# The first layer of the edge network, moved from the edge loop into the stage of the six experts

## Chip, cores and metric

One core of one Trainium2 chip runs the whole program. The metric is the device time of one execution in microseconds (us), the median of three runs.

## What is computed

The reference is a graph network of two blocks on 3125 nodes with 256 features and 50,000 edges. Block one: linear attention, six steps of a gated graph network, and six dense experts. Block two: a Galerkin-type attention beside an edge convolution, then routed experts. The change concerns one line of the edge convolution, with `ele` (50,000 x 8), `fc_w0` (8 x 64) and `fc_w1` (64 x 256) all given as inputs:

```python
hid = jax.nn.silu(edge_length_embedded @ fc_w0 / np.sqrt(NB))   # first layer
w = hid @ fc_w1 / np.sqrt(RN)                                    # second layer
wA, wB, wC, wD = (w[:, :MUL], w[:, MUL:2 * MUL], w[:, 2 * MUL:3 * MUL], w[:, 3 * MUL:])
midA = wA * xs0 * sh0          # xs0, xs1: node rows gathered by edge_src
...
y0 = jax.ops.segment_sum(mid0, edge_dst, num_segments=Nn) * inv_nb
```

`hid` depends on inputs alone, so it can be made at any time ahead of the edge loop.

## The kernel before

The program is a chain of stages, each a function with one instruction stream per engine, set down in Python order; engines meet only through semaphores (`wait_ge`, `then_inc`), and a barrier of all engines ends each stage. An engine takes its instructions strictly in order, so a wait holds up all that is queued behind it. Products that must be close to fp32 are made from two parts (`PARTS`): a high part rounded to the fast type fp32r, and the rest as a low part.

**The expert stage** (`expert_mlp`, L1686) has 42 steps `i`: seven groups of 448 nodes (`GW`) times six experts. `layer1`, `layer2` and `layer3` (L1788 to L1818) are twelve products each of 448 columns, from L1784: three combinations of parts, two halves of 256 inputs, two halves of 256 outputs. TensorE's order in a step is `layer1(i+1)`, `layer2(i)`, `layer3(i-1)` (L1826 to L1835), so each layer's result has most of a step to become the next one's operand. ScalarE takes PSUM out through relu (L1853, L1864) and makes the high part of the first hidden layer (L1857); VectorE makes the low part (L1905), scales by the gate (L1910) and splits the second hidden layer (L1915, L1917). GpSimd makes the low parts of the 18 expert matrices at the start (L1772) and is then done. After each group ScalarE copies the sum out (L1871), and TensorE turns it node by node (L1823), up to one tile of 128 nodes per step, which VectorE adds to the rows (L1960). The sync queue SP loads expert matrices (L1735), each when the one four before it has been split, and for every step the gate row spread over 128 partitions (L1745), when the scaling three steps before is done.

**The stage before it** (`gnn_to_experts`, L1464) splits the 8 edge features into parts and stores them as 24 rows, high, low, high (L1514), to `ea8_dram`. **The stage behind it** (`norm_and_galerkin`, L1970) makes among other things the first layer's weights `fw0` (L2177 to L2188).

**The edge loop** (`edge_convolution`, L2217) goes over 98 units of 512 edges, each of four chunks of 128. For a unit: SP loads 24 x 512 edge features (L2276); TensorE makes the first layer in one product of 512 columns (`hidden`, L2305), whose 128 outputs are the 64 hidden values twice; ScalarE applies silu (L2413); VectorE rounds all 128 rows (L2457) and overwrites the lower 64 with the low part (L2459). For each chunk TensorE then makes the second layer with two products of 256 columns (`weights`, L2313). GpSimd gathers 128 node rows by an indirect DMA (L2288) into one of eight buffers. VectorE multiplies gathered rows and weights (L2482, L2483), ScalarE multiplies one-hot rows of the destinations by four edge attributes (L2421), and TensorE sums over edges by products with them (`sums`, L2325 and L2328; the fp32 type makes each of these two instructions). Once per unit ScalarE copies the sums (L2428), TensorE turns them (L2336), and VectorE adds them at their nodes (L2491). TensorE's order in unit `q` is `hidden(q+2)`, and for each chunk `sums(q, j)`, `weights(q+1, j)`, with the turn of the last unit behind the second chunk.

The next stage, `route_to_blocks`, begins with a square root on ScalarE (L2695).

## Time and profile before

| | us |
|---|---|
| timed runs, median of 3 (lowest, highest) | 3843.97 (3841.3, 3848.61) |
| the profiled execution, from its first to its last instruction | 3966.1 |
| the difference of the two | 122.1 |
| expert stage, start of the first and of the last layer product | 2167.9 to 2503.6 |
| edge loop, first load issued to start of the last turn | 2647.3 to 3354.7 |

The profile shows one execution, recorded by the hardware on the core. Its clock starts at its first instruction. PE is TensorE, PEld its weight loads, DVE VectorE, ACT ScalarE, POOL GpSimd, SP the sync engine's queue; L1784 is a line of the kernel. TensorE's products are pipelined: one starts before the one ahead of it has ended, so a price is read from the distance of starts or of ends, not from a duration. A bracket with "idle before" gives the time that the engine had stood still and what ended it.

### The profile page before, as it was taken

How to read it: one execution, taken by the hardware profiler on the slowest of the kernel's cores; microseconds unless marked ns; L12 is line 12 of the kernel's file. 1: busy time of each engine (PE TensorE's matmuls, PEld its weight loads, DVE VectorE, ACT ScalarE, POOL GpSimd, SP SyncE). 2: the span in 40 equal slices, each digit the busy share in tenths (PEclk: the TensorE clock that was granted, in tenths of full speed). 3: DMA queues.
4: the chain of work that ended last, by engine and by line, in shares of the span. 5: the costliest groups of instructions: out<-in, count | busy, mean ns of one | idle time of the engine just before them, and what ended most of it. 6: DMA issues, size and time to landing. Idle time of an engine off the chain costs nothing. (4 is left out here: it accounts for less than half of the span.)

```text
span 3966.1 us, 60201 instructions
## 1 busy us (share of the span) xinstructions
PE 3642.8 (92%) x18935; PEld 3087.8 (78%) x18935; DVE 2451.9 (62%) x4843; ACT 1491.9 (38%) x3475; POOL 665.9 (17%) x658
## 2 busy tenths in 40 slices
PE   5999899999999999999996999988888888869996
PEld 2555699999999998999994888657777777848885
DVE  7886655555555555556554666556666665677775
ACT  0363311211211111112114544457777775136663
POOL 0002000000000000000002200025555553012221
PEclk9999999999999999999997999989999999879998
DMA  1353022222222222222222210112222222431113
GB/s 53 65 105 65 26 87 89 65 89 84 70 84 74 80 88 71 83 83 71 83 69 98 72 31 30 42 47 83 81 84 79 84 80 59 150 71 38 38 38 119
DMA packets 265216, 288.48 MB, mean 73 GB/s; under 512 B 70331, under 2 KB 237327, under 8 KB 264283
## 3 DMA queue, kind: packets, MB, share of 16 engines
q1 hardware_dynamic: 233701, 208.44, 18.1%
q0 software_dynamic: 24192, 66.15, 5.8%
q10 hardware_dynamic: 7030, 10.16, 0.7%
q8 instruction: 162, 2.65, 0.3%
q14 instruction: 131, 1.07, 0.1%
HBM read 242.21 MB, written 42.48 MB: 72 GB/s over the span
## 5 line engine op out<-in xcount | busy, mean ns | idle before, releaser
L1043 PE MATMUL bank<-a_wide,parts 125*128 125x448 f32 x4200 | 872.9, 367 | 0.0
L1043 PEld LDWEIGHTS bank<-a_wide,parts 125*128 125x128 f32 x4200 | 785.6, 188 | 78.4 <-issue 9.9
L2288 POOL DMA_INDIRECT rows<-h_dram,src_t x392 | 375.4, 958 | 331.9 <-DVE prod L2483 218.7
L2421 ACT ACTIVATE hot<-eq,ea 128x80 f32<-128x80 f32 x1568 | 405.3, 352 | 1.0 <-DVE eq L2463 0.5
L1093 DVE CAST a_wide<-a_cols 125x2240 fp32r<-125x2240 bf16 x210 | 275.5, 1328 | 138.7 <-PE bank L1043 138.7
L1017 POOL TENSOR_TENSOR nf_g<-nf,nf_g 128x896 fp32r<-128x896 f32 x42 | 95.4, 2271 | 1575.0 <-ACT nf_g L1187 1575.0
L2328 PEld LDWEIGHTS bank<-prod,hot 128*80 128x80 f32 x2352 | 295.9, 153 | 70.9 <-issue 21.6
L2328 PE MATMUL bank<-prod,hot 128*80 128x128 f32 x2352 | 331.8, 277 | 10.6 <-issue 10.4
L1052 PE MATMUL bank<-nf_g,whh 128*128 128x448 f32 x1512 | 339.7, 369 | 0.0
L1052 PE MATMUL bank<-msg,wc 128*128 128x448 f32 x1512 | 339.1, 369 | 0.0
L1052 PEld LDWEIGHTS bank<-msg,wc 128*128 128x128 f32 x1512 | 284.2, 188 | 27.5
L1052 PEld LDWEIGHTS bank<-nf_g,whh 128*128 128x128 f32 x1512 | 284.3, 188 | 27.4
L1192 ACT ACTIVATE msg<-bank 128x448 fp32r<-128x448 f32 x84 | 41.1, 541 | 700.7 <-PE bank L1043 700.7
L2482 DVE TENSOR_TENSOR prod<-rows,bank 128x128 f32<-128x128 f32 x392 | 111.2, 284 | 231.0 <-PE bank L2313 198.4
L2325 PE MATMUL bank<-prod,hot 128*80 128x256 f32 x784 | 240.8, 389 | 11.3 <-ACT hot L2421 7.4
L3035 DVE TENSOR_TENSOR w_up<-w,w_up 128x912 fp32r<-128x912 f32 x168 | 184.8, 1101 | 106.8 <-ACT w_up L2977 106.8
L1147 DVE TENSOR_TENSOR msg<-bank,msg 128x448 fp32r<-128x448 f32 x84 | 48.6, 620 | 306.1 <-ACT msg L1192 306.1
L2924 PE MATMUL bank<-w_up,x_t 128*128 128x456 f32 (+1 forms) x1008 | 223.2, 375 | 3.2 <-DVE w_up L3035 2.7
L1784 PE MATMUL bank<-h,ew 128*128 128x448 f32 x1008 | 214.4, 367 | 1.3 <-DVE h L1917 1.3
L2483 DVE TENSOR_TENSOR prod<-rows,bank 128x384 f32<-128x384 f32 x392 | 214.4, 547 | 0.0
L2313 PE MATMUL bank<-fw,hid 128*128 128x256 f32 x784 | 193.8, 329 | 20.7 <-DVE hid L2459 15.3
L1784 PEld LDWEIGHTS bank<-h,ew 128*128 128x128 f32 x1008 | 188.7, 188 | 19.9 <-issue 3.9
(438 smaller groups left out, 5787.7 us busy)
## 6 DMA issues: line engine op xcount, KB each, us to landing
a_cols<-a_dram SPq DMA_DIRECT2D x210, 546.9 KB
a_dram<-a_cols SPq DMA_DIRECT2D x15, 1250.0 KB, 9.9
w<-in_w SPq DMA_DIRECT2D x4, 2728.0 KB
deg_bc<-deg_dram SPq DMA_DIRECT2D x42, 224.0 KB, 6.0
gate_bc<-gate_dram SPq DMA_DIRECT2D x42, 224.0 KB, 3.2
rows<-h_dram,src_t POOLq DMA_INDIRECT x392
w<-y_rows SPq DMA_DIRECT2D x12, 512.0 KB, 15.1
w<-in_w SPq DMA_DIRECT2D x6, 896.0 KB
```

The source lines that it names most:

```text
L1043: ins = nc.tensor.matmul(p_msg[f][:, 0:GW], parts[0:SPB, m, c * HB + k, f * 128:(f + 1) * 128], a_wide[u % 2][0:SPB, k, :], start=(c == 0 ...
L1052: ins = nc.tensor.matmul(out_p[:, 0:GW], w_m[:, k, part * D + f * 128:part * D + (f + 1) * 128], x_o[:, k, :], start=(start and c == 0), s ...
L1093: nc.vector.tensor_copy(a_wide[u % 2][0:SPB, :, :], a_cols[u % 3][0:SPB, :, :]).then_inc(a_done, 1)
L1784: ins = nc.tensor.matmul(to[f][:, 0:GW], w_p[:, m, k, f * 128:(f + 1) * 128], x_p[:, i % 2, k, :], start=start and c == 0, stop=stop and c ...
L2288: nc.gpsimd.indirect_dma_start(out=rows[n % ITC][:, :], out_offset=None, in_=h_dram, in_offset=bass.IndirectOffsetOnAxis(ap=src_t[:, n:n + ...
L2313: ins = nc.tensor.matmul(p_w[j][0:EC, 0:4 * MUL], hid[:, q % 2, j * EC:(j + 1) * EC], fw1[m][:, :], start=(m == 0), stop=(m == PARTS - 1))
L2325: nc.tensor.matmul(to[:, 0:4, :], hot[:, b, j, 0, :], p[:, 0:8:2, :], start=(j == 0), stop=False, skip_group_check=True)
L2328: ins = nc.tensor.matmul(to[:, 4 + c:8:3 - c, :], hot[:, b, j, 1 + c, :], p[:, 1:4 + 2 * c:2 + 2 * c, :], start=False, stop=(j == UC - 1 a ...
L2421: ins = nc.scalar.activation(hot[:, q % 2, j, m, :], eq[:, q % 2, j, :], ACT.Copy, scale=ea4[:, q * UC + j, m:m + 1])
L2483: nc.vector.tensor_tensor(slots[:, 2:8, :].rearrange("p (c a) u -> p c a u", a=2), xs1, w_cd, ALU.mult)\
L2924: ins = nc.tensor.matmul(p_h[i][:, 0:cut.stop - cut.start], x_t[x][:, n % 2, k, :], w_up[w][:, k, cut], start=(c == 0), stop=(c == len(ter ...
L3035: nc.vector.tensor_tensor(w_up[1][:, :, cuts[i]], w13[:, bass.ds(e, 1), :, cuts[i]].rearrange("p o k n -> p (o k) n"), w_up[0][:, :, cuts[ ...
```

## The change

The first layer of all 50,000 edges is made in the expert stage and stored; the edge loop loads it.

- 98 pieces, three in each step from step 5 to step 37 of the experts: one behind `layer1`, one behind `layer2`, one behind `layer3`, on TensorE and in matching places on ScalarE. A piece is 256 columns (`HE`) of a pair of units at once: 48 input rows (two units' 8 features in three part combinations) against a weight matrix with the units' blocks apart, 128 outputs (64 hidden values of each unit).
- Each piece: three loads (16 rows of 1 KB), a product in PSUM bank 7, two silus of it on ScalarE (one rounded, one not), a subtraction on GpSimd that leaves the low part, and a 256 KB store to `hid_dram`. There are two buffers `hid` and three of `ea`. TensorE waits for the silus of the piece before, ScalarE for the store of the piece before that one.
- Bank 7 is taken from the transposes, which use bank 6 alone until the last group.
- In the edge loop `hidden`, `silu` and `split` are gone. SP loads a unit in two DMAs of 128 KB into one of seven buffers, when the second layer of seven units before has been made.
- The weights `fw0` are split on GpSimd in the expert stage; their preparation on VectorE and three memsets on GpSimd leave the stage between. The edge features are stored as 16 rows, one store of 1.5 MB fewer.
- In the adjacency builder a count is held at zero or above by one more register instruction per tile.

```diff
+HIDS = 7
+HE = 256
+PIECES = 2 * NIT
+FIRST_STEP = 5
...
-        ea8_dram = nc.dram_tensor("ea8_dram", (3 * 8, NCH * EC), F32).ap()
+        ea8_dram = nc.dram_tensor("ea8_dram", (2 * 8, NCH * EC), F32).ap()
+        hid_dram = nc.dram_tensor("hid_dram", (NIT, PARTS, 128, UE), F32).ap()
...
-            ea8 = sb(ctx, "ea8", [128, 2, UE], F32R)
-            fw0 = sb(ctx, "fw0", [128, 128], F32R)
+            hid = sb(ctx, "hid", [128, HIDS, UE], F32R)
...
                         act.reg_alu(rounds, ranges_at[t // AHEAD % 2][t % AHEAD], PACK_BITS, ALU.arith_shift_right)
-                        act.reg_add(turns, turns, rounds)
+                        act.reg_alu(more, rounds, 0, ALU.max)
+                        act.reg_add(turns, turns, more)
...
-                for at_row, part, ready in ((0, 0, ea_high), (16, 0, ea_high), (8, 1, ea_low)):
+                for at_row, part, ready in ((0, 0, ea_high), (8, 1, ea_low)):
                     sp.wait_ge(ready, START + 1)
                     sp.dma_start(ea8_dram[at_row:at_row + 8, :].rearrange("a (p n) -> (a p) n", p=EP), ea_parts[part][:, :].bitcast(F32))\
                       .then_inc(ea_stored, 16)
-                sp.wait_ge(ea_stored, START + 48)
+                sp.wait_ge(ea_stored, START + 32)
...
+        ea = [sb(ctx, f"ea{b}", [48, HE], F32R) for b in range(3)]
+        fw_raw = sb(ctx, "fw_raw", [48, 128])
+        fw_high = sb(ctx, "fw_high", [48, 128], F32R)
+        fw = sb(ctx, "fw", [48, 128], F32R)
+        hid = sb(ctx, "hid", [128, 2, PARTS, HE], F32R)
+        gate_t = hid[0:NT, :, :, :].rearrange("p b m n -> p (b m n)").bitcast(F32)[:, 0:E0 * RT].rearrange("p (e n) -> p e n", n=RT)
...
+        def piece(i, spot):
+
+            n = 3 * (i - FIRST_STEP) + spot
+            return range(n, n + 1) if 0 <= n < PIECES else range(0)
+
+        def turned_in(t):
+            return p_x[0] if t < SOON else p_x[t % 2]
+
...
+                def edges(n):
+                    if n < PIECES:
+                        i, h = divmod(n, 2)
+                        units = ea8_dram.rearrange("(m a) (i u c) -> m i u a c", m=PARTS, i=NIT, u=2)[:, i, :, :, h * HE:(h + 1) * HE]
+                        sp.dma_start(ea[n % 3][0:16, :].bitcast(F32), units[0]).then_inc(ea_in[n % 3], 16)
+                        sp.dma_start(ea[n % 3][16:32, :].bitcast(F32), units[1]).then_inc(ea_in[n % 3], 16)
+                        sp.dma_start(ea[n % 3][32:48, :].bitcast(F32), units[0]).then_inc(ea_in[n % 3], 16)
+
+                def move(n):
+                    i, h = divmod(n, 2)
+                    sp.wait_ge(hid_mm, START + n + 1)
+                    edges(n + 3)
+                    sp.wait_ge(hid_low, START + n + 1)
+                    sp.dma_start(hid_dram[i, :, :, h * HE:(h + 1) * HE].rearrange("m p e -> p m e"), hid[:, n % 2, :, :].bitcast(F32))\
+                      .then_inc(hid_out[n % 2], 16)
...
+                sp.dma_start(fw_raw[:, :], A["fw0"]).then_inc(fw_in, 16)
+                for n in range(3):
+                    edges(n)
                 for m in range(8, NM):
                     weights(m)
-                for i in range(4, NI):
-                    gate_load(i)
+                for i in range(4, NI + 4):
+                    for n in piece(i - 4, 0):
+                        move(n)
+                    if i < NI:
+                        gate_load(i)
+                    for spot in (1, 2):
+                        for n in piece(i - 4, spot):
+                            move(n)
                     if i == WKV_AT:
                         sp.wait_ge(w_low, START + NM)
                         sp.dma_start(wkv[:, :, :], A["wkv1"].rearrange("(k p) n -> p k n", p=128)).then_inc(wkv_in, 16)
+                for b in range(2):
+                    sp.wait_ge(hid_out[b], START + PIECES // 2 * 16)
 
...
+                pool.wait_ge(fw_in, START + 16)
+                nc.gpsimd.tensor_copy(fw_high[:, :], fw_raw[:, :]).then_inc(fw_step, 1)
+                pool.wait_ge(fw_step, START + 1)
+                nc.gpsimd.tensor_tensor(fw[:, :], fw_raw[:, :], fw_high[:, :], ALU.subtract).then_inc(fw_step, 1)
+                pool.wait_ge(fw_step, START + 2)
+                nc.gpsimd.tensor_copy(fw[0:32, :], fw_raw[0:32, :]).then_inc(fw_step, 1)
+                for n in range(PIECES):
+                    pool.wait_ge(silu_done, START + n + 1)
+                    nc.gpsimd.tensor_tensor(hid[:, n % 2, 1, :], hid[:, n % 2, 1, :].bitcast(F32), hid[:, n % 2, 0, :], ALU.subtract)\
+                      .then_inc(hid_low, 1)
 
...
+                def edge_layer(n):
+                    pe.wait_ge(fw_step, START + 3)
+                    pe.wait_ge(gate_done, START + 1)
+                    pe.wait_ge(ea_in[n % 3], START + n // 3 * 48 + 48)
+                    pe.wait_ge(silu_done, START + n)
+                    nc.tensor.matmul(p_hid[:, 0:HE], fw[:, :], ea[n % 3][:, :], start=True, stop=True).then_inc(hid_mm, 1)
+
                 def turn(t):
-                    pe.wait_ge(added, START + t - 1)
+                    if t < SOON:
+                        pe.wait_ge(added, START + t)
+                    else:
+                        pe.wait_ge(added, START + t - 1)
+                        pe.wait_ge(silu_done, START + PIECES)
                     for k in range(KD):
-                        ins = nc.tensor.transpose(p_x[t % 2][0:RT, k * 128:(k + 1) * 128], xt[:, k, t * RT:(t + 1) * RT], ident[:, :])
+                        ins = nc.tensor.transpose(turned_in(t)[0:RT, k * 128:(k + 1) * 128], xt[:, k, t * RT:(t + 1) * RT], ident[:, :])
                     ins.then_inc(turned, 1)
...
+                    for n in piece(i, 0):
+                        edge_layer(n)
                     if i < NI:
                         layer2(i)
+                    for n in piece(i, 1):
+                        edge_layer(n)
                     if 0 < i <= NI:
                         layer3(i - 1)
+                    for n in piece(i, 2):
+                        edge_layer(n)
...
+                def edge_layer(n):
+                    act.wait_ge(gate_out, START + 64)
+                    act.wait_ge(hid_mm, START + n + 1)
+                    act.wait_ge(hid_out[n % 2], START + n // 2 * 16)
+                    for m in range(PARTS):
+                        to = hid[:, n % 2, m, :]
+                        ins = nc.scalar.activation(to if m == 0 else to.bitcast(F32), p_hid[:, 0:HE], ACT.Silu,
+                                                   scale=8.0 ** -0.5)
+                    ins.then_inc(silu_done, 1)
...
                     if i + 1 < NI:
                         hidden1(i + 1)
+                    for n in piece(i, 0):
+                        edge_layer(n)
                     if i < NI:
                         hidden2(i)
+                    for n in piece(i, 1):
+                        edge_layer(n)
...
+                    for n in piece(i, 2):
+                        edge_layer(n)
 
...
-                for t, name in ((fw0_raw, "fw0"), (fw1_raw, "fw1"), (ea4, "ea4")):
+                for t, name in ((fw1_raw, "fw1"), (ea4, "ea4")):
                     sp.dma_start(t[:], A[name]).then_inc(edge_in, 16)
...
-                nc.gpsimd.memset(fw0[:, :].bitcast(F32), 0.0).then_inc(rest_zero, 1)
-                for n in range(2):
-                    pool.wait_ge(d_mm, START + n + 1)
-                    nc.gpsimd.memset(ea8[:, n, :].bitcast(F32), 0.0)
...
                 rounds, regs = begin(sp, "sp", per_round)
                 with sp.Fori(0, rounds) as r:
-                    units, dmas = at_round(sp, regs, per_round)
+                    chunks, = at_round(sp, regs, per_round)
                     for q in range(NU):
-                        b = q % 2
-                        sp.wait_ge(hid_mm, units + q - 1)
-                        sp.dma_start(ea8[0:24, b, :].bitcast(F32), ea8_dram[:, q * UE:(q + 1) * UE]).then_inc(ea_in[b], 16)
+                        pair, u = divmod(q, 2)
+                        sp.wait_ge(w_mm, chunks + max(q - HIDS + 1, 0) * UC)
+                        for m in range(PARTS):
+                            sp.dma_start(hid[m * MUL:(m + 1) * MUL, q % HIDS, :].bitcast(F32),
+                                         hid_dram[pair, m, u * MUL:(u + 1) * MUL, :]).then_inc(hid_in[q % HIDS], 16)
...
-                    def hidden(q):
-                        b = q % 2
-                        pe.wait_ge(ea_in[b], dmas + (q // 2) * 16 + 16)
-                        pe.wait_ge(silu_done, units + q)
-                        nc.tensor.matmul(p_hid[:, 0:UE], fw0[:, :], ea8[:, b, :], start=True, stop=True)\
-                          .then_inc(hid_mm, 1)
+                    units, chunks, loads = at_round(pe, regs, per_round)
...
-                            pe.wait_ge(hid_done, units + q + 1)
+                            pe.wait_ge(hid_in[q % HIDS], loads + q // HIDS * 32 + 32)
...
-                    def silu(q):
-                        act.wait_ge(hid_mm, units + q + 1)
-                        act.wait_ge(hid_done, units + q - 1)
-                        nc.scalar.activation(hid_raw[:, q % 2, :], p_hid[:, 0:UE], ACT.Silu, scale=8.0 ** -0.5)\
-                          .then_inc(silu_done, 1)
...
-                    def split(q):
-                        b = q % 2
-                        dve.wait_ge(silu_done, units + q + 1)
-                        dve.wait_ge(w_mm, chunks + q * UC - UC)
-                        nc.vector.tensor_copy(hid[:, b, :], hid_raw[:, b, :]).then_inc(hid_high, 1)
-                        dve.wait_ge(hid_high, units + q + 1)
-                        nc.vector.tensor_tensor(hid[64:, b, :], hid_raw[64:, b, :], hid[64:, b, :], ALU.subtract).then_inc(hid_done, 1)
...
+    fw0 = np.zeros((3, 2, 8, 2, MUL), np.float32)
+    for u in range(2):
+        fw0[:, u, :, u, :] = np.asarray(i["L1_gnn_fc_w0"])
```

## Rows read from the trace of the kernel before

**Rows 1.** The page: its first line.

```profile
span 3966.1 us, 60201 instructions
```

**Rows 2.** Busy time by windows: start:end, length, then each engine, clock, DMA share, GB/s.

```profile
2185.50:2208.40 22.90, 22.90 (x112) 20.57 (x111) 20.44 (x14) 16.70 (x27) 18.50 (x10) 1.00 0.41 116
2229.00:2480.00 251.00, 245.20 (x1205) 220.84 (x1206) 151.70 (x199) 117.41 (x176) 0.00 (x0) 1.00 0.12 35
2660.00:3350.00 690.00, 605.24 (x4364) 519.42 (x4363) 453.60 (x1161) 491.90 (x1736) 366.30 (x384) 0.98 0.28 81
```

**Rows 3.** Line L2305 (ns min/median/max, first to last start), then PE's timeline of one unit.

```profile
L2305 PE MATMUL bank<-ea,fw x98: 390/391/797, 2649.1 to 3335.4; 128*128 128x512 f32 x98
...
2867.49 0.52 PE L2313 MATMUL bank<-fw,hid 128*128 128x256 f32 x2
2867.84 0.40 PE L2305 MATMUL bank<-ea,fw 128*128 128x512 f32 x1
2868.08 0.59 PE L2325 MATMUL bank<-prod,hot 128*80 128x256 f32 x2
2868.51 0.82 PE L2328 MATMUL bank<-prod,hot 128*80 128x128 f32 x6
2869.08 0.48 PE L2313 MATMUL bank<-fw,hid 128*128 128x256 f32 x2
...
2873.67 0.40 PE L2305 MATMUL bank<-ea,fw 128*128 128x512 f32 x1
```

**Rows 4.** Timeline of the edge loop around 2905: start, length, engine, idle before.

```profile
2904.67 0.59 ACT L2428 ACTIVATE sum_rows<-bank 80x512 f32<-80x512 f32 x1 [3.59 <-DMA gate_bc<-gate_dram]
2904.71 0.29 DVE L2482 TENSOR_TENSOR prod<-rows,bank 128x128 f32<-128x128 f32 x1 [2.87 <-PE bank L2313]
...
2905.32 0.50 PE L2336 MATMUL bank<-ident,sum_rows 80*128 80x80 f32 x4 [2.00 <-ACT sum_rows L2428]
```

**Rows 5.** Timeline of the head of the edge loop.

```profile
2647.32 10.27 SPq L2276 DMA_DIRECT2D ea<-ea_dram  x5
...
2648.03 1.16 POOL L2288 DMA_INDIRECT rows<-h_dram,src_t  x1 [14.67 <-issue]
...
2653.22 2.07 PE L2313 MATMUL bank<-fw,hid 128*128 128x256 f32 x8 [3.31 <-DVE hid L2459]
...
2658.53 1.11 PE L2325 MATMUL bank<-prod,hot 128*80 128x256 f32 x2 [1.26 <-DVE prod L2483]
```

**Rows 6.** PE's timeline in the expert stage: a group's end, then one step.

```profile
2229.16 0.44 PE L1823 MATMUL bank<-ident,nf 128*128 128x128 f32 x2 [1.13 <-ACT nf L1871]
...
2302.18 5.07 PE L1784 MATMUL bank<-h,ew 128*128 128x448 f32 x24
...
2307.08 1.18 PE L1784 MATMUL bank<-x_p,ew 128*128 128x448 f32 x5
```

**Rows 7.** ACT's timeline of the same step, then two groups by line (busy us, mean ns).

```profile
2303.90 0.62 ACT L1864 ACTIVATE h_r<-bank,eb 128x448 f32<-128x448 f32 x1
...
L2699 ACT ACTIVATE xt<-bank 128x256 f32<-128x256 f32 x25 | 9.6, 383 | 20.2 <-PE bank L2669 20.2
...
L525 POOL TENSOR_TENSOR x_rows<-x_rows,bo_bc 128x256 f32<-128x256 f32 x25 | 18.2, 732 | 45.9 <-DVE xn L664 37.9 <-DMA bq<-in_L_mix_bq_t 8.0
```

**Rows 8.** Line L1905: ns min/median/max, first to last start.

```profile
L1905 DVE TENSOR_TENSOR h<-h_r,h x42: 1083/1092/2191, 2173.8 to 2491.8; 128x896 fp32r<-128x896 f32 x42
```

**Rows 9.** DMA issues from 2187 to 2205: count, KB each, median us to landing.

```profile
wkv<-in_L_ffn_expert_w SPq DMA_DIRECT2D x6, 256.0 KB, 2.8
gate_bc<-gate_dram SPq DMA_DIRECT2D x3, 224.0 KB, 3.7
```

**Rows 10.** Timelines of SP (expert stage) and of ACT (start of the route stage).

```profile
2179.12 21.26 SPq L1735 DMA_DIRECT2D wkv<-in_L_ffn_expert_w  x10
...
3430.82 1.28 ACT L2695 ACT_TABLE_LOAD   x1 [76.45 <-PEq L108]
```

**Rows 11.** Group by line, whole program: busy us, mean ns, idle before and what ended it.

```profile
L2313 PE MATMUL bank<-fw,hid 128*128 128x256 f32 x784 | 193.8, 329 | 20.7 <-DVE hid L2459 15.3 <-issue 5.3
```

84 lines of the change are left out of this document (33 added, 51 removed).

## The prediction

> **What bounds the kernel now.** I read the windows of the two stages that change, then the PE timeline inside one turn of each, then who waits in them. TensorE is the limit in both. In the expert stage it is busy 245.2 of 251.0 us, with ACT at 117.4, VectorE at 151.7 and GpSimd idle [rows 2]. Its products follow each other without a gap: 24 products of 448 columns begin at 2302.18 and the next group at 2307.08, 0.204 us each, so a step of 36 takes 7.35 us [rows 6]. The only regular hole is 1.13 us once in six steps, where a transpose waits for ScalarE to copy the finished group out [rows 6].
>
> The edge loop looks less clear: 605 of 690 us busy [rows 2], and its 98 units start 7.08 us apart (2649.1 to 3335.4 over 97 intervals) [rows 3]. But a unit in which nothing waits takes 5.83 us (2867.84 to 2873.67) [rows 3]. What fills the difference is odd: at 2904.7 ScalarE and VectorE end idle times of 3.59 and 2.87 us within 0.04 us of each other, both put down to products or sums that TensorE had behind it for two microseconds and more, and TensorE, out of work, then starts 0.6 us later [rows 4]. 97 intervals times 1.25 us are 121 us. The profiled execution spans 3966.1 us [rows 1], the median of the timed runs is 3844.0: a difference of 122.1 us. I take these holes for something that only the profiled execution has, and the loop of the timed runs for bound by TensorE at 5.83 us per unit. That is an inference from two sizes that agree; the rival below drops it.
>
> **The change, part by part.** The sum is made on the profiled execution and carried to the median, since every term is read from stretches without those holes.
>
> **(a) The 512-column product leaves the loop.** Ends are what count on a pipelined engine: the pair before it ends at 2867.49 + 0.52 = 2868.01, the product at 2868.24, so it costs 0.23 us [rows 3]. 96 lie in the steady loop: 96 x 0.23 = **-22.1 us**. The bound from below is 0, if another engine limits. With it go ScalarE's silu, VectorE's two splitting instructions and their waits, all off the path in a unit of 5.83. What is next: GpSimd was busy 366.3 us with 384 gathers, 0.95 us each, 3.8 us for the four of a unit, and ScalarE 491.9 us, 5.1 per unit with the silu in it [rows 2]; the new unit is 5.60, so both stay hidden.
>
> **(b) Head of the loop.** Before, the load is issued at 2647.32, the second layer starts at 2653.22 and the first sums at 2658.53 [rows 5]: load, product, table load, silu, split, twice over. Now there are two loads. A 256 KB load takes 2.8 us from issue to landing [rows 9], so weights start near 2650.4; their eight products take 2.07 us [rows 5], the first gather was issued at 2648.03 [rows 5], and sums can start near 2653. I take **-5.5 us**; the low end is 2.3, where gathers hold the loop back once the weights are there, the high end 6.
>
> **(c) 98 products of 256 columns enter the expert stage,** three per step. The nearest row is the pair with 256 columns of the same type in the loop: the sums before it end at 2868.51 + 0.82 = 2869.33, the pair at 2869.56, 0.115 us each [rows 3]. 98 x 0.115 = **+11.3 us**. The ends: 0.16 by their starts (0.32 to the next group, halved) and 0.23 as for 512 columns, so 11.3 to 22.5. They hold half the columns of what leaves, since a product now makes the layer of two units at once. One in each of six groups falls into the 1.13 us hole: **-0.7**.
>
> **(d) What rides along in a step.** ScalarE gets six activations of 256 columns, 0.38 us each [rows 7], 2.3 us on top of 3.6 of 7.7. VectorE gets nothing. GpSimd gets three subtractions of 0.73 [rows 7]. I price all three at 0, for this cover: from 2185.5 to 2208.4, while weights were split, GpSimd was busy 18.5 of 22.9 us and ScalarE 16.7, and TensorE was busy all 22.9 [rows 2]. In that stage a VectorE subtraction took up to 2.19 us where its median is 1.09 [rows 8]: the engines hold each other up, and TensorE did not feel it. The Trainium skill says why (SBUF — State Buffer, Who interferes with whom): a GpSimd instruction and a VectorE one with two SBUF inputs take turns on one port pair, each for its whole length. By that rule three subtractions could stretch VectorE's 4.7 us per step by 2.2, to 6.9 of 7.7, which would still be hidden.
>
> **(e) The sync queue.** Per piece three small loads and a store, in front of and behind the gate loads. The store of a piece is issued before the next gate load in the first spot; in the others it comes behind that load's wait, when GpSimd has only just finished. Priced at 0. At the start ten issues (weights and nine loads) stand ahead of the loads of expert weights from 2179.12 on, which follow as splits are done [rows 10]. Ten at about 0.3 us delay them by 3 us; with a start of supply as tight as this, TensorE may feel 0 to 3: I take **+1.5 us**.
>
> **(f) Tables.** Silu leaves the edge loop, so ScalarE can keep the square-root table to the next stage, whose first instruction is a 1.28 us load with everybody behind it [rows 10]: **-1.3 us**. The one in the expert stage has slack. The smaller preparation in the stage between, the dropped store of 1.5 MB long before its stage ends, and one register instruction per tile in an adjacency builder where ScalarE waits for TensorE: 0 each.
>
> **Sum:** -22.1 - 5.5 + 11.3 - 0.7 + 1.5 - 1.3 = -16.8 us. 3844.0 - 16.8 = **3827.2 us**.
>
> **Rivals.**
> *The ring of two buffers (slower).* A buffer is free for the next but one piece when its store has landed. In microseconds from the start of a first layer (2299.7, twelve products ahead of 2302.18): ScalarE's copy ends and the next instruction starts at 4.2 [rows 7], and two silus end at 4.9; GpSimd, if it is held up by VectorE's subtraction as that is by GpSimd's [rows 8], begins at 5.5 and ends at 6.2; the store, 256 KB, lands 2.8 later [rows 9], at 9.05. Only then the step's third silu runs (it was ready at 7.9), and behind it queue two relus, the copy and the next step's silus, which end at 12.4. TensorE wants that bank at 7.7 + 5.0 = 12.7. So 0.3 us is to spare, and every microsecond more of landing goes whole into each of 33 steps. At the 3.7 us of the gate load in the same stretch [rows 9] that is 0.6 x 33 = 20 us, and with a silu or a subtraction 0.2 longer 26: 3844 - 17 + 26 = 3853. Against it: the load of the same size and packet took 2.8, and this stage moves little else. For: no store was seen. It decides from a landing of about 3.1 us. Chance 0.14.
>
> *The loop is not TensorE's (no change).* If the holes are real in timed runs, or gathers or waits on VectorE set the unit, (a) is worth nothing: 3827.2 + 22.1 = 3849. For: 7.08 is what the trace shows. Against: the 122 us. Chance 0.14.
>
> *More is gained (faster).* In the loop TensorE stood idle 20.7 us ahead of the second layer, most of it for the split hidden layer [rows 11]; loaded seven units ahead, that wait is gone. If those waits are in timed runs too, 15 us more: 3812. Chance 0.08.
>
> *Dear products (within the noise):* half the columns may not mean half the time; at 0.23 each (c) doubles and the result is 3838. Chance 0.06. My forecast keeps 0.58.
>
> **How the numbers follow.** The forecast's own range is -25 to -8 us, from (b)'s and (e)'s ends and 0.115 to 0.16 in (c): 3819 to 3836. To leave out no more than 2 in 10 it has to take in the no-change rival and the cheap half of the ring: 3817 to 3850. A measurement can tell 0.2%, 7.7 us. Faster by more: nearly all of the forecast, the bigger gain, 0.65. Within: the no-change rival, the dear products, a mild ring, 0.20. Slower: the ring in full or two rivals together, 0.15.
>
> **What would show it.** Right: in a step of experts the 448-column products keep their 0.204 us and three 256-column ones stand between with no idle time before them; steps lengthen by 0.35 us; the shortest unit of the loop is 5.60 us; first sums near 5.5 us after the first load; no table load in the loop or ahead of the route stage. Wrong: TensorE idle before a 256-column product, released by ScalarE's silu, whose own idle time ends with a landing store (the ring); or units whose shortest length stays at 5.8 (another bound, GpSimd's gathers first). A PE hole near 2190 longer than 3 us would say that the queue was dearer than (e).

## The result and the profile after

The changed kernel takes 3896.45 us (median of 4 runs, 3895.25 to 3900.0), the kernel before 3844.27 beside it (3841.3 to 3848.61): a ratio of 1.0138, 95% interval 1.0124 to 1.0152. It is slower by 52 us, where 17 us less was forecast and 3817 to 3850 was the range.

TensorE's time from its first to its last instruction of each stage says where (us, from the traces; the loop's is from the issue of its first load). The last column is the kernel before with one small edit ("The bank in the kernel before" below), whose profiled execution had no holes in the edge loop.

| stage | before | changed | difference | before with one edit |
|---|---|---|---|---|
| norm and attention | 147.7 | 151.3 | +3.6 | 147.8 |
| gated graph | 1619.6 | 1618.6 | -1.0 | 1617.7 |
| experts | 341.9 | 420.0 | **+78.1** | 376.8 |
| edge loop | 779.3 | 628.1 | see below | 653.9 |

The attention stage isn't touched; in the other kernels of this study it took 147.3 to 151.3 us with the same code, so its 3.6 us are scatter. The expert stage is the loss. The loop's own gain has to be read against a profile without holes, 653.9 us: 25.8 us.

The page's first line and its DMA issues of the changed kernel, then two windows (start:end, length, each engine's busy time, clock, DMA share, GB/s), one in the expert stage and one in the loop:

```profile
span 3893.5 us, 60754 instructions
...
hid_dram<-hid SPq DMA_DIRECT2D x98, 256.0 KB, 2.8
hid<-hid_dram SPq DMA_DIRECT2D x196, 128.0 KB, 3.1
```

```profile
2229.00:2480.00 251.00, 231.93 (x1014) 183.92 (x1013) 131.68 (x158) 137.13 (x289) 75.07 (x75) 0.98 0.38 122
2760.00:3300.00 540.00, 538.54 (x4213) 486.93 (x4212) 361.80 (x943) 430.43 (x1581) 347.55 (x368) 1.00 0.47 134
```

The span, 3893.5, and the profiled execution's time, 3895.25, are those of the timed runs: there are no holes this time, and TensorE is busy 538.5 of 540 us of the loop. The stores land in the 2.8 us of [rows 9]. In the expert stage TensorE now does 1014 matrix instructions in the 251 us in which it did 1205 [rows 2], and its clock is 0.98.

TensorE's timeline over two steps of the expert stage of the changed kernel (start, length, line, operation, count, idle before) answers to [rows 6]:

```profile
2307.18 0.41 PE L1893 MATMUL bank<-ident,nf 128*128 128x128 f32 x2 [0.70 <-DVE x_rows L2052]
2307.35 2.70 PE L1843 MATMUL bank<-x_p,ew 128*128 128x448 f32 x12
2309.97 0.38 PE L1884 MATMUL bank<-ea,fw 48*128 48x256 f32 x1
2310.29 2.72 PE L1843 MATMUL bank<-h,ew 128*128 128x448 f32 x12
2312.93 0.38 PE L1884 MATMUL bank<-ea,fw 48*128 48x256 f32 x1
2313.25 2.72 PE L1843 MATMUL bank<-h,ew 128*128 128x448 f32 x12
2315.89 0.38 PE L1884 MATMUL bank<-ea,fw 48*128 48x256 f32 x1
...
2318.57 0.41 PE L1893 MATMUL bank<-ident,nf 128*128 128x128 f32 x2 [2.29 <-DVE x_rows L2052]
2318.73 4.15 PE L1843 MATMUL bank<-x_p,ew 128*128 128x448 f32 x12
```

Three things are to be seen. Groups of twelve begin 2.94 and 2.96 us apart (2307.35, 2310.29, 2313.25), where twelve products are 12 x 0.204 = 2.45: a piece costs 0.49 us and not 0.115. PE shows no idle time at it, because the product's modelled length covers the gap; only the starts tell. Ahead of the transposes TensorE waits for VectorE's addition (L2052), 21.9 us in all; in the kernel before that wait was 0.4 us, once, behind the last group. And after the longest of these waits the next twelve products take 4.15 us in place of 2.70. By line, the pieces and the transposes of the changed kernel, with what ended the idle times ahead of them:

```profile
L1884 PE MATMUL bank<-ea,fw x98: 352/382/536, 2219.7 to 2543.6; 48*128 48x256 f32 x98
its engine sat idle before it (us, times) until:
  issue: 32.5, 98
  ACT hid L1949: 1.3, 2
...
L1893 PE MATMUL bank<-ident,nf x50: 272/286/447, 2236.6 to 2586.4; 128*128 128x128 f32 x50
its engine sat idle before it (us, times) until:
  issue: 25.9, 17
  DVE x_rows L2052: 21.9, 15
  ACT nf L1957: 13.6, 14
```

The ring of two buffers, the rival that I feared, is not it: TensorE waited 1.3 us for silus, in two places.

### The profile page after: what moved, and what is told of

It is laid out like the page before. It is cut to its first block and busy times, and to the rows that moved or that the text cites. A ratio compares the mean times of both kernels' runs of the same rounds, so it can differ in the third digit from the quotient of the medians.

```text
span 3893.5 us, 60754 instructions
## 1 busy us (share of the span) xinstructions
PE 3632.3 (93%) x18935; PEld 3072.4 (79%) x18935; DVE 2381.3 (61%) x4644; ACT 1501.7 (39%) x3572; POOL 760.4 (20%) x756
## 5 line engine op out<-in xcount | busy, mean ns | idle before, releaser
L2402 PE MATMUL bank<-prod,hot 128*80 128x128 f32 x2352 | 321.9, 273 | 0.0
L1843 PE MATMUL bank<-h,ew 128*128 128x448 f32 x1008 | 225.3, 373 | 2.5 <-DVE h L2009 2.5
L2973 PEld LDWEIGHTS bank<-w_up,x_t 128*128 128x128 f32 x1008 | 186.6, 190 | 20.1 <-issue 3.0
```

Of the source, the lines that this page charges most:

```text
L1843: ins = nc.tensor.matmul(to[f][:, 0:GW], w_p[:, m, k, f * 128:(f + 1) * 128], x_p[:, i % 2, k, :], start=start and c == 0, stop=stop and c ...
L2402: ins = nc.tensor.matmul(to[:, 4 + c:8:3 - c, :], hot[:, b, j, 1 + c, :], p[:, 1:4 + 2 * c:2 + 2 * c, :], start=False, stop=(j == UC - 1 a ...
L2973: ins = nc.tensor.matmul(p_h[i][:, 0:cut.stop - cut.start], x_t[x][:, n % 2, k, :], w_up[w][:, k, cut], start=(c == 0), stop=(c == len(ter ...
```

## The experiments

All ratios are to the kernel before in runs of the same session. "Stage" is the expert stage as in the table: 341.9 before, 420.0 changed.

**Rows.** Every tile of the piece's product is made 128 high; rows 48 on are zeroed once.

```diff
-        ea = [sb(ctx, f"ea{b}", [48, HE], F32R) for b in range(3)]
-        fw = sb(ctx, "fw", [48, 128], F32R)
+        ea = [sb(ctx, f"ea{b}", [128, HE], F32R) for b in range(3)]
+        fw = sb(ctx, "fw", [128, 128], F32R)
...
+                for t in (fw, *ea):
+                    nc.gpsimd.memset(t[:, :].bitcast(F32), 0.0).then_inc(zeroed, 1)
```

> The changed kernel, with each piece's product made over 128 rows in place of 48: the tiles of edge attributes and of the weight are 128 rows high, the rows from 48 on are set to zero once before the first load, and the loads still bring 48 rows. The result is the same. In the trace of the changed kernel a step with a piece between two groups of the first and second layer takes 2.95 us from group to group in place of 2.45, so a piece costs 0.49 us and not the 0.115 that I put into the sum. Theory of the rows: a product of 48 rows stands between products of 128 rows, its weight is loaded only when the product before it has ended, and the next weight of 128 rows only when it has ended itself, so that nothing overlaps. Then 128 rows bring the piece to 0.12 us: 98 x 0.37 = 36 us less, 3860 us. Theory of the waits: the four waits ahead of each piece take the sequencer the time, and rows don't matter: 3896 us, and the groups stay 2.95 us apart.

3885.66 us, 1.0110 (1.0093 to 1.0127); stage 406.2. Only 11 us less, not 36. Its timeline shows that the piece's price fell as the rows theory says, and what took its place:

```profile
2340.46 2.61 PE L1847 MATMUL bank<-x_p,ew 128*128 128x448 f32 x12
2342.90 0.27 PE L1888 MATMUL bank<-ea,fw 128*128 128x256 f32 x1
2343.02 2.60 PE L1847 MATMUL bank<-h,ew 128*128 128x448 f32 x12
```

```profile
L1888 PE MATMUL bank<-ea,fw 128*128 128x256 f32 x94 | 28.2, 300 | 7.3 <-ACT hid L1953 7.1
L1897 PE MATMUL bank<-ident,nf 128*128 128x128 f32 x50 | 10.9, 308 | 37.2 <-DVE x_rows L2056 29.6 <-ACT nf L1961 7.2 <-issue 0.3
```

These groups stand 2.56 us apart (2.59 in the median), 0.12 or a little more for a piece. But TensorE now gets to the transposes sooner and waits there 29.6 us for VectorE, and 7.1 for silus: the second and third cause were hidden behind the first.

**Waits.** Two of the four waits ahead of a piece only ahead of the first.

```diff
-                    pe.wait_ge(fw_step, START + 3)
-                    pe.wait_ge(gate_done, START + 1)
+                    if n == 0:
+                        pe.wait_ge(fw_step, START + 3)
+                        pe.wait_ge(gate_done, START + 1)
```

> The changed kernel, with 48 rows as it has, and two of TensorE's four waits ahead of each piece (for the split weight and for the gates) made only ahead of the first. Theory of the rows: nothing changes, 3896 us. Theory of the waits: half of 98 x 0.37 us goes, 3878 us.

3895.34 us, 1.0132 (1.0116 to 1.0149); groups 2.96 us apart as before. Two waits fewer changed nothing, so the number of waits is not the cause.

**One bank.** The transposes go behind the next first layer.

```diff
-                    for t in turns(i):
-                        pe.wait_ge(y_out, START + (i - 1) // E0 * KD)
-                        turn(t)
                     if i + 1 < NI:
                         layer1(i + 1)
+                    for t in turns(i):
+                        pe.wait_ge(y_out, START + (i - 1) // E0 * KD)
+                        turn(t)
```

> The changed kernel, with the transposes of the results (two to a step, all into bank 6 since the pieces took bank 7) issued behind the next first layer, 2.9 us later in the step, in place of ahead of it. In the changed kernel TensorE stood 21.9 us in 15 of these steps for VectorE's addition of the tile before. Theory of the bank: VectorE makes that addition 1.2 to 1.5 us into the next step, the transposes' new place lies behind it, and the idle time goes: 22 us less, 3874 us. Theory of the late VectorE: the steps are as long as VectorE or ScalarE need in them, and TensorE's wait only moves to the second layer or to the next products: 3896 us, within 3 us.

3864.86 us, 1.0052 (1.0035 to 1.0069); stage 389.3, 30.7 less, more than the 22 us of the wait; with the waits also went the four stretches at a lower clock behind them, some 5.6 us. What is left over the stage of before is 47.4 us, 98 pieces at 0.48.

**Both.**

> Both edits of the two other kernels: 128 rows and the transposes behind the first layer. If the rows and the bank are the two missing terms and don't overlap, 36 and 22 us go: 3838 us, a little under the kernel before (3844). If with the shorter step another engine becomes the bound (ScalarE's work in a step with three pieces: two products' activations and copies of some 4.2 us and six silus of 0.38 us, 6.5 us against a step of 7.7; VectorE's 5.4), less goes: 3850 or more.

3851.82 us, 1.0020 (1.0010 to 1.0030); stage 375.7. The rows again gave 13 us only. TensorE waited 14.0 us for silus, and those for the stores, which stand behind loads on the sync queue. By line, then the queue's timeline (start, time to issue):

```profile
L1953 ACT ACTIVATE hid<-bank 128x256 fp32r<-128x256 f32 (+1 forms) x190 | 62.6, 382 | 76.6 <-DMA hid_dram<-hid 67.8 <-PE bank L1888 8.7
...
L1888 PE MATMUL bank<-ea,fw 128*128 128x256 f32 x94 | 29.9, 319 | 14.2 <-ACT hid L1953 14.0
```

```profile
2345.07 0.60 SPq L1773 DMA_DIRECT2D ea<-ea_dram  x1
2345.71 0.60 SPq L1774 DMA_DIRECT2D ea<-ea_dram  x1
2346.35 0.59 SPq L1775 DMA_DIRECT2D ea<-ea_dram  x1
2346.99 0.41 SPq L1782 DMA_DIRECT2D hid_dram<-hid  x1
```

Each 16 KB load takes 0.60 us to issue, and there is no space between: the queue issues for 2.4 us per piece, against 2.57 of TensorE. Once a step it also stands for VectorE's scaling ahead of the gate load (27.9 us in 32 times), and then it is behind.

**Two loads.** Attributes of both units, first and second part, come in one load of 32 rows; the weight's rows are reordered to match.

```diff
-                        sp.dma_start(ea[n % 3][0:16, :].bitcast(F32), units[0]).then_inc(ea_in[n % 3], 16)
-                        sp.dma_start(ea[n % 3][16:32, :].bitcast(F32), units[1]).then_inc(ea_in[n % 3], 16)
+                        both = ea8_dram.rearrange("b (i u c) -> i u b c", i=NIT, u=2)[i, :, :, h * HE:(h + 1) * HE]
+                        sp.dma_start(ea[n % 3][0:32, :].bitcast(F32), both).then_inc(ea_in[n % 3], 16)
```

> The kernel with 128 rows and the later transposes (3852 us), with the attributes of a piece brought by two loads (32 rows and 16) in place of three (16 each); the rows of the weight are put in the order that this needs. The result is the same. In that kernel ScalarE's silus stood for the stores of the pieces, and the sync queue was full: in a step with three pieces nine loads of 0.60 us to issue, three stores of 0.41 and a gate row of 0.35 are 7.0 us of the step's 7.9. Theory of the full queue: with six loads of 0.6 it is 5.2 us, the stores go out as soon as they are ready, the waits of TensorE for the silus (14 us) go, and the time falls to 3838 to 3842 us. Rival, the ring of two buffers itself: a store takes 2.8 us to land whatever the queue does, and the piece after next waits for it: within 3 us of 3852.

3836.81 us, 0.9977 (0.9967 to 0.9987); stage 360.7, 15 us less. Waits for silus 2.1 us:

```profile
L1953 ACT ACTIVATE hid<-bank 128x256 fp32r<-128x256 f32 (+1 forms) x190 | 62.6, 383 | 55.2 <-DMA hid_dram<-hid 45.2 <-PE bank L1888 8.6
...
L1888 PE MATMUL bank<-ea,fw 128*128 128x256 f32 x95 | 29.9, 315 | 2.6 <-ACT hid L1953 2.1
```

The queue was the limit for TensorE, and not the ring by itself: ScalarE still stands 45.2 us for stores, but TensorE hardly notices. The stores show the queue's slack: with three loads they stood 12.2 us in all for GpSimd's subtraction, with two 51.4, so now the queue is there first.

**How many rows.** The same kernel with tiles of 64 and of 96 rows.

> As the kernel with two loads and 128 rows, but the tiles of the pieces' product are 64 rows high. If the product costs by its rows (each row short of 128 leaves the array something to wait for), the groups of a step with a piece stand between 2.57 us (128 rows) and 2.95 us (48 rows) apart, at about 2.85. If it is a matter of a bound at 64 rows, they stand 2.95 us apart as with 48 rows, and the time is 15 to 30 us over that with 128 rows; or, if 64 rows are still free, 2.57 us and no difference.

> As the kernel with two loads and 128 rows, but 96 rows. If the price goes by the rows, about 2.7 us from group to group and 98 x 0.12 = 12 us over the kernel with 128 rows. If there is a bound at 64 rows: as with 128 rows, 2.57 us from group to group, and the same time.

64 rows: 3862.12 us, 1.0044 (1.0027 to 1.0061), stage 384.6. 96 rows: 3837.69, 0.9984 (0.9974 to 0.9993), stage 362.3, as with 128. TensorE's timeline with 64 rows, then with 96, each followed by the piece's weight load (PEld):

```profile
2339.76 2.72 PE L1847 MATMUL bank<-h,ew 128*128 128x448 f32 x12
2342.41 0.38 PE L1888 MATMUL bank<-ea,fw 64*128 64x256 f32 x1
2342.72 2.72 PE L1847 MATMUL bank<-h,ew 128*128 128x448 f32 x12
...
2342.41 0.18 PEld L1888 LDWEIGHTS bank<-ea,fw 64*128 64x128 f32 x1 [0.32 <-issue]
```

```profile
2343.14 2.71 PE L1847 MATMUL bank<-h,ew 128*128 128x448 f32 x12
2345.68 0.28 PE L1888 MATMUL bank<-ea,fw 96*128 96x256 f32 x1
2345.80 1.39 PE L1847 MATMUL bank<-x_p,ew 128*128 128x448 f32 x6
...
2345.49 0.19 PEld L1888 LDWEIGHTS bank<-ea,fw 96*128 96x128 f32 x1
```

With 64 rows the next group starts 0.31 us behind the piece and 2.96 behind the group before, as with 48; with 96 it starts 0.12 behind the piece. So the price steps somewhere above 64 rows and by 96, and isn't proportional to the rows. The weight loads show where the time goes: with 96 rows the piece's weight is loaded from 2345.49 on, beside the product ahead of it, 0.2 us before the piece starts at 2345.68. With 64 rows the weight loads stand still for 0.32 us, and the piece's starts only with the piece itself, at 2342.41. This is in line with the Trainium skill (TensorEngine Tiling (Array Packing), Tiling Modes), by which a change of the tiling mode drains the engine; its modes have 128, 64 or 32 rows. That the array changed its mode here is an inference; no run shows the mode.

**The loop alone.** Only the first pair's two pieces are made; 96 are left out, and the loop loads the first pair's result each time (so the results of the other 48 pairs are missing).

```diff
-PIECES = 2 * NIT
+PIECES = 2
...
-                                         hid_dram[pair, m, u * MUL:(u + 1) * MUL, :]).then_inc(hid_in[q % HIDS], 16)
+                                         hid_dram[0, m, u * MUL:(u + 1) * MUL, :]).then_inc(hid_in[q % HIDS], 16)
```

> The changed kernel with only the two pieces of the first pair made in the expert stage; the other 96 (their loads, products, silus, subtractions and stores) are left out, and the edge loop loads the first pair's result for every pair. The edge loop does all that it does in the changed kernel. So this prices the change without what it puts into the expert stage, but for the transposes' one bank. By my parts (a), (b) and (f) the loop, its head and the table load give 28.9 us: 3844 - 29 = 3815 us, and 3837 at most if the transposes' wait on one bank (22 us, which counts VectorE's place in steps lengthened by the pieces) is there in full without the pieces too. If the expert stage is back at 342 us and the time is 3844, the loop had gained nothing in the timed runs.

3853.20 us, 1.0021 (1.0011 to 1.0030). That looks as if the loop had gained nothing, and it fell outside both numbers of my theory. The stages tell: experts 378.8, 36.9 over before with almost no piece in them. 3853.2 - 36.9 = 3816.3, the 3815 expected. The single bank costs 37 us, not 22.

**The bank in the kernel before.** One bank for the transposes, nothing else of the change (a count in an early stage is held at zero or above, as in the changed kernel).

```diff
-                    pe.wait_ge(added, START + t - 1)
+                    pe.wait_ge(added, START + t - (t >= SOON))
-                        ins = nc.tensor.transpose(p_x[t % 2][0:RT, k * 128:(k + 1) * 128], xt[:, k, t * RT:(t + 1) * RT], ident[:, :])
+                        ins = nc.tensor.transpose(p_x[t % 2 if t >= SOON else 0][0:RT, k * 128:(k + 1) * 128], xt[:, k, t * RT:(t + 1) * RT], ident[:, :])
...
-                        nc.vector.tensor_tensor(x_rows[:, t, :], x_rows[:, t, :], p_x[t % 2][0:RT, 0:D], ALU.add).then_inc(added, 1)
+                        nc.vector.tensor_tensor(x_rows[:, t, :], x_rows[:, t, :], p_x[t % 2 if t >= SOON else 0][0:RT, 0:D], ALU.add).then_inc(added, 1)
```

> The kernel before, with nothing of the change but the transposes' single bank: for the tiles that are turned one to a step, the transposes go to bank 6 alone and wait for VectorE's addition of the tile just before (in place of the one before that). Bank 7 stands empty. If the bank alone does it, the expert stage goes from 341.9 us to the 378.8 us of the kernel with the loop alone, and the time to 3844 + 37 = 3881 us. If the bank costs only in steps that the pieces have shifted, under 10 us more.

3876.43 us, 1.0094 (1.0078 to 1.0109); stage 376.8, +34.9. TensorE at its longest wait, then VectorE's addition and what it did just ahead of it, then a window, whose third figure from the end is the granted clock:

```profile
2352.25 0.59 PE L1825 MATMUL bank<-ident,nf 128*128 128x128 f32 x2 [2.69 <-DVE x_rows L1962]
2352.49 4.17 PE L1786 MATMUL bank<-x_p,ew 128*128 128x448 f32 x12
```

```profile
2350.69 1.08 DVE L1902 TENSOR_TENSOR x_p<-nf,x_p 128x896 fp32r<-128x896 f32 x1
2351.69 0.41 DVE L1962 TENSOR_TENSOR x_rows<-x_rows,bank 128x256 f32<-128x256 f32 x1
```

```profile
2350.00:2355.00 5.00, 2.75 (x9) 2.52 (x10) 2.71 (x5) 0.00 (x0) 0.00 (x0) 0.73 0.19 45
```

The transposes of a tile want VectorE's addition of the tile before, and VectorE makes it last in its step, behind the second layer's split and once a round also behind the split of the next rows (L1902). 26.3 us of waits stand in the trace. Five times the wait was 2.69 us, and behind four of these the twelve products took 4.05 to 4.24 us rather than 2.69 while the clock was lower (0.73 in the window above, 1.00 in the five microseconds before it), 5.8 us in all; behind the fifth, at 2404.98, they took 2.69. 26.3 + 5.8 = 32 of the 35 us; the other 3 are not accounted for.

This run also shows the loop of before without holes: 538.5 of 540 us busy in the same window, and a span of 3871.3 beside a time of 3873.26.

**The removed product, put back.** Into the kernel with two loads, in 96 units.

```diff
+                        if q + 2 < NU:
+                            pe.wait_ge(hid_in[(q + 2) % HIDS], loads + (q + 2) // HIDS * 32 + 32)
+                            nc.tensor.matmul(bank[0][:, 0:UE], fw1[0][:, 0:128], hid[:, (q + 2) % HIDS, :], start=True, stop=True)
```

> The kernel with 128 rows, later transposes and two loads, with a product of 128 rows and 512 columns put back into each of 96 units of the edge loop, where the removed one stood: its operands are the loaded hidden values and the first 128 columns of the second weight, and its result goes to a bank that nobody reads. It prices part (a) by itself. If TensorE sets the loop's pace with nothing idle (part (a)): 96 x 0.23 = 22.1 us more, 3859 us. If the loop waits elsewhere in the timed runs, under 10 us more. If the product costs more in its place than its 512 columns, as the pieces did, over 30 us more.

3859.81 us, against 3836.81 without it in another session: +23.0, or 27 by the two ratios (1.0048 and 0.9977), since the kernel before was 3.5 us quicker in this one. By the traces TensorE's time in the edge stage went from 624.4 to 647.0: 22.6 us. Part (a) stands. These two kernels have the same expert stage, and it took 360.7 us in one trace and 363.9 in the other: a difference of 3 us between two stages is not clear of scatter.

**A piece twice.** The product of each piece issued two times.

```diff
+                    nc.tensor.matmul(p_hid[:, 0:HE], fw[:, :], ea[n % 3][:, :], start=True, stop=True)
                     nc.tensor.matmul(p_hid[:, 0:HE], fw[:, :], ea[n % 3][:, :], start=True, stop=True).then_inc(hid_mm, 1)
```

> The kernel with 128 rows, later transposes and two loads, with each piece's product of 256 columns issued twice in a row into the same columns of the bank. It prices one product of 256 columns once the rows are right: 98 x 0.115 = 11.3 us more by part (c), 3848 us. If a product between others of its kind of rows still costs what the space between the groups showed (2.57 us against 2.45, 0.12 us) the same comes out; if a product of another weight costs 0.23 us whatever its columns: 22.5 us more.

3837.37 us, 0.9990 (0.9981 to 1.0000), below what either theory gave. Stage 367.4, 6.7 more than 360.7 (3.5 more than 363.9), and the groups are 0.10 us further apart (2.67 for 2.57):

```profile
2360.39 0.28 PE L1888 MATMUL bank<-ea,fw 128*128 128x256 f32 x1
2360.51 0.29 PE L1889 MATMUL bank<-ea,fw 128*128 128x256 f32 x1
2360.63 2.60 PE L1847 MATMUL bank<-x_p,ew 128*128 128x448 f32 x12
```

So a product of 128 rows and 256 columns costs 0.12 us in its place. The median rose by 0.6 us, or 5 by the two ratios, where 98 x 0.115 is 11.3; TensorE's waits in the stage were some 2 us shorter, and the rest is not explained.

**Behind the second layer, the store first.** The transposes move to the place behind `layer2(i)`, and in `move` the store is issued ahead of the loads.

```diff
                 def move(n):
                     i, h = divmod(n, 2)
-                    sp.wait_ge(hid_mm, START + n + 1)
-                    edges(n + 3)
                     sp.wait_ge(hid_low, START + n + 1)
...
+                    sp.wait_ge(hid_mm, START + n + 1)
+                    edges(n + 3)
```

> The kernel with 128 rows and two loads (3837 us), with the transposes moved once more, from behind the first layer to behind the second, and each piece's store issued ahead of the loads for the piece after the next two. In that kernel TensorE still stood 5.9 us for VectorE's additions and 2.6 us for silus in the expert stage. Theory: both are waits for work that ends a little late, and both go: 8 us less, 3829 us, about what my sum gave for the change. Rival: ScalarE's and VectorE's chain of the second layer is what the step waits for then, and the time only moves: within 2 us of 3837.

3847.88 us, 1.0019 (1.0010 to 1.0029), stage 374.0: worse by 13. The transposes' wait went (1.5 us left), but the loads, which now stand behind the wait for GpSimd's subtraction, came late:

```profile
L1888 PE MATMUL bank<-ea,fw 128*128 128x256 f32 x94 | 28.9, 308 | 19.4 <-DMA ea<-ea_dram 19.1
```

**Bias rows.** The kernel just above, with the 14 bias products (18 rows) padded to 128 as the pieces are.

```diff
-        b3 = sb(ctx, "eb3", [3 * E0, D], F32R)
+        b3 = sb(ctx, "eb3", [128, D], F32R)
-        share = [sb(ctx, f"share{b}", [3 * E0, GW], F32R) for b in range(2)]
+        share = [sb(ctx, f"share{b}", [128, GW], F32R) for b in range(2)]
-                for t in (fw, *ea):
+                for t in (b3, *share, fw, *ea):
```

> The kernel with the transposes behind the second layer, with the products that add the third layer's bias (18 rows, 448 columns, two for each of seven groups, in the kernel before too) padded to 128 rows by zero rows. If few rows cost a product what they cost the pieces, about 0.37 us for each row of two that stand together: 7 x 0.37 = 2.6 us less than the kernel with the transposes behind the second layer; up to 5.2 if each of the two pays. If the cost of the pieces was not their rows but something else that the padding also changed, nothing.

3845.90 us, 1.0014 (1.0004 to 1.0023); stage 370.8. By its time alone inconclusive, so both were tried again with the loads first:

> 128 rows, two loads, and the transposes behind the second layer, but each piece's loads ahead of its store again, as in the changed kernel. In the kernel with the store first TensorE stood 19.1 us for the late loads of edge attributes and 1.5 us ahead of the transposes; in the one with the transposes behind the first layer 2.6 us for silus and 5.9 us ahead of the transposes. If both readings hold, only about 4 us of waits are left: 4 us less than with the transposes behind the first layer (3837 us), 3833 us, an expert stage of 356 to 358 us on TensorE. If the transposes' place makes no difference, 3837 us and 361 us.

3832.20 us, 0.9974 (0.9965 to 0.9983); stage 358.5. The stage is 15.5 us shorter than with the store first. Against the transposes behind the first layer (0.9977, stage 360.7) the difference is within the scatter.

> As the kernel of this call with the loads first, with the 14 products of 18 rows that add the third layer's bias padded to 128 rows. With the store first the same edit took the expert stage from 374.0 to 370.8 us. If few rows are what costs, 2.6 to 3.2 us less again: 3830 us. If that difference was the late loads' chance, none.

3828.20 us, 0.9961 (0.9947 to 0.9974); stage 356.4. This is the best version, 0.4% under the kernel before. The bias rows took 2.1 us off the stage and 4.0 off the median, where 2.6 to 3.2 were expected. Neither is clear of scatter. In the trace itself the group behind a bias pair starts 0.48 us after it rather than 0.60, and the pair 0.23 us behind the piece ahead rather than 0.29: 7 x 0.17 = 1.2 us, in the expected direction and under half of its size.

## Why the prediction was wrong

The steps, each with what it measured:

- **(a), right.** 22.1 us said; 22.6 by putting the product back, and 5.81 against 5.58 us per unit.
- **(b), right in kind, a little too large.** 11.4 us from the first load's issue to the first sums in the kernel before with one edit (2678.46 to 2689.86), 7.21 in the changed one (2727.50 to 2734.71): -4.2, not -5.5. Fourteen loads are issued there one behind another, 0.64 us apart. The second half of the first unit is issued 0.6 us after the first and landed in 3.2 us, where I had taken 2.8 for the whole, and the sums then stood 1.26 us for ScalarE's one-hot rows.
- **(c), the step that failed.** "98 x 0.115": the nearest row [rows 3] was of products with 128 rows, and I matched columns and type and left out the rows. They were in the code (48), and a row of their kind was in the trace of before, which I didn't read: the two bias products of 18 rows, behind which the next group starts 0.61 us later, where two of 128 rows would take 2 x 0.204 = 0.41. From TensorE's timeline of the kernel before:

```profile
2187.99 0.67 PE L1813 MATMUL bank<-share,eb 18*128 18x448 f32 x2
2188.60 2.71 PE L1784 MATMUL bank<-h,ew 128*128 128x448 f32 x12
```

  The piece measured 0.49, 98 of them 48 us, 37 more than said; at 96 or 128 rows it is 0.12 as said. My rival of dear products, 0.23 by its columns, was too cheap by half for the same reason.
- **The second step that failed: a term that was not in the sum.** The diff gives bank 7 to the pieces and so puts the transposes on one bank, with a wait for the addition just made. I gave it no price, and never asked where in its step VectorE issues the addition. It costs 35 to 37 us alone, and 27 in the changed kernel (the sum below).
- **(d), half right.** No engine became the bound by its busy time. But the rule of the Trainium skill that I weighed (SBUF — State Buffer, Who interferes with whom), by which the two engines share a port pair that one of them holds at a time, does act. The trace agrees with it in kind, though not in who pays: VectorE's two-input instructions that overlapped a subtraction (L1997, L2002) kept their 1092 ns, and GpSimd's subtraction took 1090 ns in the median where I had 732, while VectorE's copy (L2007) went from 627 to 1037 ns in the mean. Those 0.4 us per step sit ahead of the addition that the transposes wait for. What they cost there was not measured by itself: the bank costs as much with no subtraction at all (stage 376.8).
- **(e), the start right, the rest wrong.** The sixth first-layer group starts 40.16 us after the first in the changed kernel and 37.89 before: +2.3, said 1.5 (0 to 3). The steady state was priced at 0 without counting issue times, and the small loads that I took "at about 0.3 us" are 0.60 each. The queue was then full, and it cost 15 us once the first two causes were gone.
- **(f), right.** No table load is ahead of the route stage any more: from the end of the edge loop to the route stage's first product TensorE's gap went from 6.67 to 5.39 us, 1.3 less.
- **The ring**: stores land in 2.8 us, as said. In the changed kernel ScalarE stood 7.5 us for them, in ten places, at most 2.2, and TensorE 1.3 for its silus.
- **The holes**: an inference then, borne out now. The same loop without them is 125 us shorter, and time and span agree within 2 us in all later profiles. (ScalarE's row in [rows 4] names a DMA as what ended its wait, and not a product as I wrote; its instruction waits for the sums.)
- **The range**: "-25" was not what its own terms give. With (b) at 6, (c) at 0.115 and (e) at 0 the sum is -18.8, so the forecast's own low end was 3825 us and not 3819. It didn't matter here, where the result lies on the other side.

The sum again, of measured parts: -25.8 for the loop and its head, -1.3 for the table load, +48 for the pieces, +36 for the bank, +2.3 at the start give +59; the kernel shows +52. The overlap is between the pieces and the bank. With the pieces in the step the waits for VectorE's addition are shorter, 0.70, 2.29 and 1.29 us in place of 0.90, 2.69 and 1.68. In the changed kernel's own trace the expert stage adds up: 48 for the pieces, 21.5 for the waits, 5.6 for the lower clock behind four of them, 1.3 for silus, 2.3 at the start, and 1.9 less of waiting for ScalarE's copied sums, 77 of the measured 78. With the causes removed the stage went 420.0, 389.3 (transposes later), 375.7 (rows), 360.7 (loads), 358.5, 356.4, where the last two steps are within the scatter. The best version is 15 us under the kernel before by its ratio, but it also pads the bias rows, which are no part of the change. Without that it is 10 us (0.9974; 7 to 13 by the interval) of the forecast 17.

## What to carry to other kernels

A product's price is read from a row with the same number of rows as well as columns, by the start of what follows it: 48 or 64 rows among products of 128 cost four times what 96 or 128 do, with no idle time of PE in the profile, only 0.32 us ahead of the weight load. When a diff takes a buffer or bank from a step that it doesn't otherwise touch, look up when the awaited instruction is issued on its engine; moving the waiting step by a third of a step took the price away. And remove causes together: taken by itself first, the largest one looked like 11 us.

## What the runs showed of the hardware that was not expected

- The step in price between 64 and 96 rows: 0.49 to 0.12 us at 256 columns, with the weight load beside the product ahead at 96 rows and behind it at 64.
- The clock can fall behind a short wait. In the changed kernel TensorE was idle 2.29 us ahead of 2318.57; a microsecond later its granted clock was 0.50, the lower of its levels (1.2 GHz), until 2323, and was 1.00 (2.4 GHz) again after that. Behind the waits of 1.29 us the next twelve products took their 2.70 us. It is not certain either: TensorE stood 2.28 or 2.29 us five times, and behind four of them the next twelve products took 3.98 to 4.24 us, behind the one at 2439.68 they took 2.68. Windows of the first case, then products of the other:

```profile
2320.00:2323.00 3.00, 3.00 (x9) 2.20 (x8) 0.00 (x0) 0.72 (x2) 0.00 (x0) 0.51 0.30 100
2323.00:2326.00 3.00, 3.00 (x14) 2.40 (x14) 1.09 (x1) 2.65 (x6) 0.84 (x1) 1.00 0.04 11
...
2439.68 0.41 PE L1893 MATMUL bank<-ident,nf 128*128 128x128 f32 x2 [2.28 <-DVE x_rows L2052]
2439.98 2.68 PE L1843 MATMUL bank<-x_p,ew 128*128 128x448 f32 x12
```

- A load of 16 KB in 16 rows takes the sync queue 0.60 us to issue, a store of 256 KB 0.41: what fills the queue is the number of transfers, not their bytes.
- One profiled execution of a kernel can hold 122 us that none of its timed runs has.

What stays open: why the full 98 x 0.37 us never showed in one step (64 to 128 rows gave 24 us of the stage, and 7 us of new waits), why one wait in five left the clock alone, and how the loads at the head of the loop hold each other up.
